# A two-layer recurrent and attention kernel: the order ahead of attention, four recurrence units, and three loops written out

## What is computed

```python
x = L0_attn_h                                   # (8, 512, 256)
xn = layernorm(x)
s = two_gated_scans(xn)                         # first layer: minGRU-like
g = silu(top1_expert_ffn(xn))                   # routed to one of 8 experts
x = x + s * g
xn = layernorm(x)
# second layer, branch s: a recurrence over time with a 16x16 state per head
xx = shift(xn); dx = xx - xn; lerp = xn + dx * xw
r = (xn + dx * lora_r(lerp)) @ rW.T             # likewise k, v, g
w = exp(-exp(lora_d(xn + dx * lora_d(lerp))))
def step(st, (rt, wt, kt, vt)):
    kv = outer(kt, vt)
    y = einsum('bhi,bhij->bhj', rt, st + u * kv)
    return wt * st + kv, y
s = (silu(g) * layernorm_per_head(ys)) @ oW.T
# second layer, branch f: attention with rotary positions, then 8 experts (top 2) and a shared one
h = xn + attention(rmsnorm(xn))                 # 16 heads of 64, causal, latent keys and values
f = h + moe(rmsnorm(h))
out = x + s * silu(f)
```

## Time and profile before

| | us |
|---|---|
| three timed runs | 2396.13, 2400.5, 2401.87 |
| their median | 2400.5 |
| the profiled run | 2402.85 |
| its span (first to last instruction) | 2401.0 |
| mean granted clock of TensorE | 0.942 of full speed |

### The profile page before, as it was taken

One profiled execution on the slowest core, in us unless ns is written; L12 is line 12 of the kernel. 1 busy time (PEld: TensorE's weight loads), 2 busy tenths in 40 slices (PEclk: granted clock), 3 DMA queues, 4 the chain that ended last, 5 costly groups with the idle time before them and its releaser, 6 DMA issues.

```text
span 2401.0 us, 40186 instructions
## 1 busy us (share of the span) xinstructions
PE 2101.0 (88%) x11714; PEld 1263.1 (53%) x11715; DVE 1798.9 (75%) x2984; ACT 957.0 (40%) x2514; POOL 829.8 (35%) x666
## 2 busy tenths in 40 slices
PE   7996899995898988998898989898988988898987
PEld 4553799983355445544553454455445544553454
DVE  6996566652796888778777967896888778787966
ACT  3453344430273237234612641273237134512641
POOL 1336000001553353235324532543353235324520
PEclk9998899995999999999999989999999999999998
DMA  6553421113122122112202220231122122202210
GB/s 170 166 146 132 124 56 53 55 51 96 53 67 58 33 52 63 41 47 51 76 14 62 54 68 5 62 72 54 33 52 63 41 54 48 72 14 62 58 41 9
DMA packets 145782, 151.74 MB, mean 63 GB/s; under 512 B 47664, under 2 KB 105648, under 8 KB 145584
## 3 DMA queue, kind: packets, MB, share of 16 engines
q1 hardware_dynamic: 138288, 136.73, 21.2%
q0 software_dynamic: 3072, 8.41, 1.1%
q10 hardware_dynamic: 4224, 4.19, 0.6%
HBM read 121.71 MB, written 27.43 MB: 62 GB/s over the span
## 4 chain that ended last, share of the span: by engine, by line
PE 48%; DVE 13%; issue 11%; ACT 2%; POOL 2%; DVEq 0%; DMA 0%; ACTq 0%; POOLq 0%
PE bank L1357 17%; PE bank L1161 11%; PE bank L1218 4%; PE bank L1235 3%; DVE arena L1743 3%; PE bank L1272 3%; PE bank L1370 2%; DVE arena L1756 2%; DVE arena L1763 2%; PE bank L1245 2%; POOL arena L2020 1%; PE bank L1182 1%; PE bank L1221 1%; PE bank L1297 1%; ACT arena L1549 1%
## 5 line engine op out<-in xcount | busy, mean ns | idle before, releaser
L2020 POOL TENSOR_TENSOR arena<-arena 128x512 f32<-128x512 f32 x256 | 344.2, 1349 | 709.1 <-DVE arena L1763 617.1
L1357 PE MATMUL bank<-arena 128*128 128x512 f32 (+2 forms) x1312 | 443.7, 493 | 13.1 <-DVE arena L1889 5.5
L1161 PE MATMUL bank<-arena 128*128 128x512 f32 (+2 forms) x768 | 372.4, 631 | 18.8 <-DVE arena L1680 10.3
L1763 DVE TENSOR_TENSOR_SCAN arena<-arena 128x512 f32<-128x512 f32 x256 | 345.5, 1350 | 16.1 <-issue 14.1
L1357 PEld LDWEIGHTS bank<-arena 128*128 128x128 f32 x1312 | 253.9, 208 | 196.2 <-issue 150.2
L1549 ACT ACTIVATE arena<-bank,arena 128x128 f32<-128x128 f32 (+3 forms) x512 | 266.6, 531 | 191.5 <-DVE arena L1743 185.6
L1756 DVE TENSOR_TENSOR arena<-arena 128x512 f32<-128x512 f32 x256 | 234.1, 914 | 50.9 <-DMA arena<-values 44.7
L1161 PEld LDWEIGHTS bank<-arena 128*128 128x128 f32 (+2 forms) x768 | 143.1, 196 | 218.5 <-issue 178.0
L1218 PE MATMUL bank<-arena 64*128 64x128 f32 (+3 forms) x1024 | 207.5, 482 | 48.1 <-ACT arena L1549 46.0
L1743 DVE TENSOR_REDUCE arena<-bank 128x2 f32<-128x256 f32 (+3 forms) x256 | 207.2, 809 | 40.4 <-PE bank L1221 40.2
L1558 ACT ACTIVATE arena<-bank 128x128 f32<-128x128 f32 (+3 forms) x512 | 197.2, 441 | 89.9 <-PE bank L1235 89.4
(11 more groups left out here) (205 smaller groups left out, 2928.9 us busy)
## 6 DMA issues: line engine op xcount, KB each, us to landing
arena<-values SPq DMA_DIRECT2D x256, 256.0 KB, 3.5
arena<-in_L_attn_h SPq DMA_DIRECT2D x16, 512.0 KB, 3.9
arena<-in_W1T SPq DMA_DIRECT2D x8, 1024.0 KB, 5.0
arena<-in_W2T SPq DMA_DIRECT2D x8, 1024.0 KB, 8.7
sorted_rows<-arena SPq DMA_DIRECT2D x42, 128.5 KB, 10.1
arena<-sorted_rows SPq DMA_DIRECT2D x40, 128.5 KB, 2.1
arena<-in_b2row SPq DMA_DIRECT2D x40, 128.0 KB, 2.9
gate_rows<-arena SPq DMA_DIRECT2D x39, 128.0 KB, 1.7
```

What stands on the lines that cost most here:

```text
L1161: last = nc.tensor.matmul(dst[rows, :], w, x, start=(n == 0), stop=(n == len(pairs) - 1))
L1357: last = nc.tensor.matmul(dst[o], w, x, start=first, stop=last_one)
L1763: nc.vector.tensor_tensor_scan(state[n % STATES][:, 1:T + 1], proj["w"][:, m, :], kv[n % 2], VEC["init"][:, m * HD + j:m * HD + j + 1], AL ...
L2020: nc.gpsimd.tensor_tensor(prods[(n + 2) % PRODS], state[n % STATES][:, 0:T], proj["r"][:, m, :], ALU.mult).then_inc(prod_done, 1)
```

## The change

It has five parts, all in `phase_c`:

- On PE, ACT and DVE the loop over seven passes is written out. POOL and SP keep their loops.
- PE: the transposes of xb go ahead of gate products 0; the keys and queries 0 and 1 go ahead of gate products 1 and product g. ACT copies xb ahead of r, and DVE turns keys and queries 0 and 1 ahead of the gate rows 1 and the residual.
- DVE has two units ahead of attention (`AHEAD` = 2) where it had six. Attention has units 2 to 19 in its steps (`STEPPED` = 20); units 20 to 23 stand behind the last step. In `experts` unit 27 moves from the beginning of what stands there to behind the first expert.
- POOL: the addition of the keys goes ahead of the products, of which two stand before the queries' additions, not four.
- SP stores the output behind copy 8, not behind copy 5.

```diff
-AHEAD = 6
+STEPPED = 20
+AHEAD = 2
...
-    for n in range(AHEAD, EARLY):
+    for n in range(AHEAD, STEPPED):
...
-QKV = "q0 q1 sp0 sp1 lat q2 q3 q4 q5 q6 q7".split()
+QKV = "sp0 sp1 lat q2 q3 q4 q5 q6 q7".split()
...
-        ("pr_r0", "a"), ("pr_r1", "a"), ("xb0", "a"), ("xb1", "a"), ("pr_g0", "a"), ("pr_g1", "a"), ("ckv", "v")]
-       + [(x, "v" if x[0] in "qs" else "a") for x in QKV])
+        ("xb0", "a"), ("xb1", "a"), ("pr_r0", "a"), ("pr_r1", "a"), ("ckv", "v"), ("q0", "v"), ("q1", "v"),
+        ("pr_g0", "a"), ("pr_g1", "a")] + [(x, "v" if x[0] in "qs" else "a") for x in QKV])
...
-                    if n == COPIES + 1 and not first:
+                    if n == 2 * COPIES and not first:
                         store_sequence(b - 1)
...
+                pe.wait_ge(xb_done, b + 1)
+                for k in range(KD):
+                    turn(bank[pre.bank(f"xb{k}")], lambda i: xb[:, i, k * P:(k + 1) * P], f"xb{k}", b, pre, pre_read, made)
                 if ended is not None:
                     gates(ended, 0)
                 project(b, "r")
+                pe.wait_ge(a_read, pre.read(b, "xb1"))
+                product(b, "ckv", [(kva_w[:, k, :], xbT[:, k, :]) for k in range(KD)])
+                query(b, 0)
+                query(b, 1)
                 if ended is not None:
                     gates(ended, 1)
-                pe.wait_ge(xb_done, b + 1)
-                for k in range(KD):
-                    turn(bank[pre.bank(f"xb{k}")], lambda i: xb[:, i, k * P:(k + 1) * P], f"xb{k}", b, pre, pre_read, made)
                 project(b, "g")
-                pe.wait_ge(a_read, pre.read(b, "xb1"))
-                product(b, "ckv", [(kva_w[:, k, :], xbT[:, k, :]) for k in range(KD)])
...
                 result(b, "var0", [(full, mean_m, sq[0], True, True)], bank[post.bank("var0")])
+                reduce_state(b, STEPPED // 4)
...
-            with pe.Fori(0, B - 1) as b:
+            for b in range(B - 1):
...
-                unit(b, 1, 2)
-                unit(b, 2, 2)
-                v.wait_ge(a_read, pre.read(b, "pr_r1"))
-                for m in range(KD):
-                    state_input(m)
-                scan(b, 3)
-                if ended is not None:
-                    gate_rows(ended, 1)
-                    residual(ended)
-                outer(b, 5)
-                scan(b, 4)
-                outer(b, 6)
-                scan(b, 5)
...
+                scan(b, 1)
+                v.wait_ge(a_read, pre.read(b, "pr_r1"))
+                for m in range(KD):
+                    state_input(m)
                 rotate(0)
+                rotate(1)
+                rotate(2)
+                if ended is not None:
+                    gate_rows(ended, 1)
+                    residual(ended)
...
-                scan(b, EARLY)
+                for n in range(STEPPED, EARLY - 1):
+                    unit(b, n)
+                scan(b, EARLY - 1)
                 scale_values(b, GROUPS - 1)
                 center()
-                outer(b, EARLY + 1)
-                unit(b, EARLY + 1)
+                outer(b, EARLY)
+                unit(b, EARLY)
...
             def experts(b, final):
+                unit(b, EARLY + 1)
                 unit(b, EARLY + 2)
-                unit(b, EARLY + 3)
...
                 def between(e):
+                    if e == 0:
+                        unit(b, EARLY + 3)
...
-                g.wait_ge(a_read, pre.read(b, "pr_r1"))
-                for n in range(STATES):
-                    product(b, n)
                 for n in range(1 + NH // 2):
+                    if n == 1:
+                        g.wait_ge(a_read, pre.read(b, "pr_r1"))
+                        for k in range(AHEAD):
+                            product(b, k)
...
-                product(b, EARLY)
-                product(b, EARLY + 1)
+                for n in range(STEPPED, EARLY + 1):
+                    product(b, n)
```

More of the change, by code:

```diff
@@ L1190, in project, with query @@
                     product(b, f"pr_{x}{m}", [(rkvg_w[x][:, k, m * P:(m + 1) * P], src[:, k, :]) for k in range(KD)])
+            def query(b, i):
+                product(b, f"q{i}", [(q_w[:, k, i * P:(i + 1) * P], xbT[:, k, :]) for k in range(KD)])
             def fold(half):
@@ L1337, in before_attention @@
                     if name[0] == "q":
-                        product(b, name, [(q_w[:, k, i * P:(i + 1) * P], xbT[:, k, :]) for k in range(KD)])
+                        query(b, i)
                         if name in ("q5", "q6"):
@@ L1388, in attention @@
                         spread_inverse(b, (i - GSTEPS - 4) // GSTEPS)
-                    for g in range(EARLY // 4):
+                    for g in range(STEPPED // 4):
                         if i == UNIT_STEP[4 * g + 3] + 3:
                             reduce_state(b, g)
-                for g in range(EARLY // 4):
+                for g in range(STEPPED // 4):
                     if UNIT_STEP[4 * g + 3] + 3 > PSTEPS + LAG:
@@ L1530, in before_attention @@
                     nc.scalar.activation(proj["w"][:, m, :], proj["w"][:, m, :], ACT.Exp, scale=-1.0).then_inc(w_step, 1)
-                copy("r")
                 for k in range(KD):
                     take(b, f"xb{k}", xbT[:, k, :], ACT.Copy, scale=VEC["w_ln1"][:, k:k + 1]).then_inc(a_read, 1)
+                copy("r")
                 if ended is not None:
@@ L1616, in _ @@
             attention(0)
-            with act.Fori(0, B - 1) as b:
+            for b in range(B - 1):
                 experts(b, False)
@@ L1810, in before_attention @@
                     gate_rows(ended, 0)
-                outer(b, 2)
-                unit(b, 1, 2)
-                unit(b, 2, 2)
-                v.wait_ge(a_read, pre.read(b, "pr_r1"))
-                for m in range(KD):
-                    state_input(m)
-                scan(b, 3)
-                if ended is not None:
-                    gate_rows(ended, 1)
-                    residual(ended)
-                outer(b, 5)
-                scan(b, 4)
-                outer(b, 6)
-                scan(b, 5)
                 def rotate(n):
@@ L1837, in rotate @@
                         nc.vector.tensor_tensor(shuf[n % 2][0:rows, :], shuf[n % 2][0:rows, :], sin[0:rows, :], ALU.mult).then_inc(rope_dve, 1)
-                rotate(0)
+                outer(b, 2)
+                scan(b, 1)
+                v.wait_ge(a_read, pre.read(b, "pr_r1"))
+                for m in range(KD):
+                    state_input(m)
+                rotate(0)
+                rotate(1)
[3 more added lines that the diff above has]
+                    residual(ended)
                 for name in QKV:
@@ L1977, in _ @@
             attention(0)
-            with v.Fori(0, B - 1) as b:
+            for b in range(B - 1):
                 experts(b, False)
@@ L2055, in attention @@
                         widen(i // GSTEPS - 1)
-                    for n in [n for n in range(STATES, EARLY) if UNIT_STEP[n] == i]:
+                    for n in [n for n in range(AHEAD, STEPPED) if UNIT_STEP[n] == i]:
                         product(b, n)
-                product(b, EARLY)
-                product(b, EARLY + 1)
+                for n in range(STEPPED, EARLY + 1):
+                    product(b, n)
                 g.wait_ge(v_read2, post.read(b, "mean0"))
@@ L2063, in experts @@
             def experts(b, final):
+                product(b, EARLY + 1)
                 product(b, EARLY + 2)
```

## The result

The changed kernel takes 2305.25 us (median of four runs, 2302.97 to 2306.85), the kernel before 2398.32 in the same comparison. The ratio is 0.9616, with a 95% interval of 0.9593 to 0.964: 92 us less. The profiled run took 2302.97 us with a span of 2301.1; that of the kernel before had a span of 2401.0. The forecast was 2307.

A forecast was written before the change was run, and what follows sets the result against it. TensorE, busy 88% of the span, was taken as the bound, losing time to waits and half clock. Gains of 55.5 + 17 + 20.4 + 0 = 93 us gave a forecast of 2307 us, range 2282 to 2334.

The forecast's parts named there:

- wait before the latent: TensorE's eight waits for the turned keys, one a sequence, ahead of attention: all 55.5 us go, with 4.4 us of cover.
- clock behind it: Queries after the latent run at a fuller TensorE clock: 2.1 us a sequence, 17 us in all.
- units to the end of attention: Three more VectorE units, 6.8 us, fit the idle time before the last scaling: cost 0, 1.3 to 2.8 us over.
- reduction of units 20 to 23 behind `var0`: TensorE's reduction leaves attention for a gap where TensorE waits anyway: 0.6 us a sequence gained.
- loops: Writing out the loops on TensorE, ScalarE and VectorE removes the jumps: 20.4 us gained, lower bound 15.4.
- reduction of units 24 to 27: In the experts, TensorE waits for VectorE's one extra unit before this reduction: 0.6 us a sequence lost.
- order and store: Keys and queries ahead of g help remove the 55.5 us wait before the latent; the store's move counts 0.
- Rival 1: VectorE and GpSimd set the pace from the latent on, so the clock brings nothing: 2324 us; chance 0.14.
- rival 2: Three units don't fit before the last scaling, as GpSimd blocks VectorE's outer products on shared ports: 2314 us; chance 0.09.
- Rival 3: At the experts' start, the reduction and no jump may keep TensorE's clock up: 2280 us; chance 0.10.
- rival 4: TensorE's written-out code arrives too late, 62 packets at up to 3.1 us each: 2497 us; chance 0.03.

The follow-up runs named there:

- e7: The changed kernel with the first read_out on VectorE placed behind the last row maxima instead of one step ahead of them: 2277.98 us.
- e6: The changed kernel with TensorE's reduction of units 20 to 23 after the gate product at the experts' start instead of behind `var0`: 2319.45 us.
- e5b: The changed kernel with all three loops over the sequences (TensorE, ScalarE, VectorE) put back: 2342.93 us.
- e1: The kernel before with only the three loops over the sequences (TensorE, ScalarE, VectorE) written out: 2381.8 us.
- e8: The kernel before with the four units moved and the three loops written out, keys, queries and store as before: 2298.98 us.
- e9: e8 with the first read_out placed behind the last row maxima: 2281.09 us.
- e3: The kernel before with only the four units moved from ahead of attention to its end, with the reduction of units 20 to 23: 2346.64 us.
- e4: The kernel before with only the order of keys and queries changed as in the changed kernel; units, loops and store as before: 2366.66 us.

## Why the prediction was right, by its own steps

| term | predicted | measured |
|---|---|---|
| wait before the latent | 55.5 | 51.7 (H to L, and the first sequence) |
| clock behind it | 17 | about 30 |
| units to the end of attention | 0 | 29 lost by the read_out's place (e7) |
| reduction of units 20 to 23 behind `var0` | 5 | not measured against its old place; 12 against one behind the gate product (e6) |
| loops | 20.4 | 38 (e5b), 18 alone (e1) |
| reduction of units 24 to 27 | 5 lost | 2.0 of waits |
| order and store | part of the first row | no gain seen beside the units (e8, e9) |

The terms of this list are taken apart one at a time from a kernel in which they act on each other, so their sum need not be 92.

**The wait** went wholly, with 6.6 us of cover where 4.4 were predicted. The cause as told was only half right: the prediction has the keys ahead of g and the units out of the way work together. The units do it alone (e3); the order alone moves the wait to the scores (e4).

**The clock behind it** was mis-sized. The step that took 2.1 us a sequence from the distance between VectorE's turns left out the latent itself (1.91 us before, 1.07 now) and stayed under its own upper bound for the sixteen instructions (9.98 - 7.0 = 3.0; measured 9.98 - 7.14 = 2.84). 0.84 and 2.84 are 3.7 us a sequence, 29.4 in all if the eight are alike. L to T bears this out: it gains 35.8 us from the kernel before to e7, where nothing is lost to the read_out, and 8.6 of those are the reduction (8 x 1.07) that has left attention, which leaves 27.2. Rival 1, that VectorE's pace swallows the gain, did not happen.

**The four units at the end of attention** fit, as predicted: VectorE keeps 1.9 us of idle time a sequence, and 1 to 3 were forecast. The scans there run at up to 2.18 us where one alone takes 1.28 (at 1343.30, in the same sequence). GpSimd's products run beside them, as in these two rows of sequence 3:

```profile
1356.93 1.64 POOL L2026 TENSOR_TENSOR arena<-arena 128x512 f32<-128x512 f32 x1 [2.90 <-DVE arena L1770]
...
1357.47 2.18 DVE L1770 TENSOR_TENSOR_SCAN arena<-arena 128x512 f32<-128x512 f32 x1
```

So the contention of rival 2 is there, but not its price. The Trainium skill (SBUF — State Buffer, "SBUF: two separate sides") says that whichever of the two engines starts first has the shared ports for its whole instruction, and that the other fully blocks. Here the scan is 0.9 us longer, and the product still had 1.1 us to run when it began, which about agrees. **The step that failed** is this one of the prediction: "Inside attention it has 18 units before and after." The count is right, and I stopped at the count. What else is tied to the numbers of those units, the read_out, moved by four units' worth of steps to the one place in attention where VectorE's delay reaches TensorE. That cost 29 us in the changed kernel and stood nowhere, in no rival either.

**The loops.** 20.4 us was read as the difference between a stretch with the jump and one without in the trace of before, and e1 confirms it (18) for that kernel. That the price would be the same in the changed kernel was taken without a reason, and it failed: there it is 38. Some 11 of the 20 us are longer stops that leave no wait behind, the rest goes with the clock. Rival 3, "a reduction in that gap and no jump may keep it up", had a chance of 0.10 and 27 us. It came true in part: the experts opened at 1.00 in three of seven sequences and at 0.86 in one. The gain of 28.3 us in T to H doesn't show it by itself, as the loops alone gain 25.4 there; but the changed kernel has done seven reductions of 1.07 more in that stretch. With the reduction elsewhere no sequence reads 1.00 (e6). With the read_out out of the way six of seven do (e7), and 2278 us lies below the range that was given, 2282.

**Slower code fetch**, rival 4, was not seen: the "issue" waits at the transposes are gone, and the instruction queue moved fewer packets than before, 83 against 96.

So it is luck that the total came so close: a loss of 29 us that was missed stood against gains of about the same size that were missed, about 12 in the clock behind the latent and 18 in the loops.

## What to carry to other kernels

When a table of steps is shifted, list everything that is placed by an expression over that table, not only the entries, and look in the trace at what each one is now in front of. Price a stop of TensorE together with the clock of what follows it, and ask what other work or wait the changed kernel would have in its place: the same jump was worth 18, 38, 44 and 47 us in four versions of one kernel. Parts that remove the same wait must not be added up, and a part that is worth nothing in the whole may be worth 20 us alone; other parts bring more together than apart.

## What the runs showed of the hardware

At the end of attention TensorE's idle times, none of them over 1.75 us, went with a granted clock well under full, and a delay of 0.6 us among them was worth 29 us of a program of 2300 (e7 and the changed kernel). The windows at that place in sequence 3:

```profile
1352.00:1359.00 7.00, 4.67 (x52) 3.63 (x53) 6.05 (x7) 3.83 (x13) 2.73 (x2) 0.67 0.20 62
```

```profile
1341.00:1348.00 7.00, 4.86 (x64) 2.92 (x64) 6.66 (x9) 4.62 (x13) 2.73 (x2) 1.00 0.29 72
```

The first window is the changed kernel's, the second that of e7. Sequence 3 is a clear case and not the rule for every one. With the idle time at about 1.15 us such a window reads 1.00 in four sequences of e7 and about 0.8 in the other four, and in the kernel before 1.00 in three of eight and about 0.8 in five; with 1.75 us it reads 0.6 to 0.8 in all eight of the changed kernel. But e5b has the 1.75 us too, and in its last three sequences the clock stayed at 1.00 all the same, as here:

```profile
1805.19 0.65 PE L1276 MATMUL bank<-arena 128*32 128x128 f32 x16 [1.74 <-ACT arena L1565]
...
1807.92 0.86 PE L1276 MATMUL bank<-arena 128*32 128x128 f32 x24 [1.28 <-ACT arena L1565]
```

So the low clock is more frequent behind the longer wait, but this wait alone doesn't bring it about. That the same code opened the experts at 1.00 in some sequences and at 0.72 in others of one execution I had not expected either; what decides between them in the changed kernel stays open.
